# Value products of four tiles in one visit, with the side work set in another order

## What is computed

```python
x = x + tanh(g_xattn) * xattn(layernorm(x), ctx, mask)
x = x + tanh(g_ffn)   * ffn(layernorm(x))
...
q, k, v = proj(hs, Wq, bq), proj(at, Wk, bk), proj(at, Wv, bv)   # 16 heads of 16
probs = softmax(clip(where(attend, q @ k.T / 4, -10000), -50, 50))
delta = layernorm(rs * ((probs @ v) @ Wo.T + bo)) * gamma + beta
...
h = silu(bitlinear(x, w1)) * bitlinear(x, w2)                    # width 704
return bitlinear(h, w3)       # bitlinear: rows of the activations rounded to 8 bits, weights ternary
```

## Time and profile before

| what | value |
|---|---|
| median of 3 runs | 1528.89 us (1526.29 to 1529.96) |
| the profiled execution: its own time | 1529.9 us |
| its span, first to last instruction | 1528.1 us, mean granted TensorE clock 0.973 |
| busy in the span: TensorE, weight loads, VectorE, ScalarE, GpSimd | 91%, 80%, 75%, 64%, 29% |
| one batch in the middle (from the scores behind the value products of n = 5 to the same place one batch on) | 44.87 us |

### The profile page before, as it was taken

How to read it: one execution, slowest core, us unless ns; L and a number is a source line. 1 busy time by engine, 2 the same in 40 slices (tenths; PEclk the granted TensorE clock), 3 DMA queues, 4 the chain that set the end, 5 groups by cost and what they waited for, 6 DMA issues and landing times. The chain is left out here.

```text
span 1528.1 us, 48034 instructions
## 1 busy us (share of the span) xinstructions
PE 1394.8 (91%) x19984; PEld 1219.7 (80%) x19984; DVE 1147.5 (75%) x2241; ACT 979.4 (64%) x1634; POOL 444.9 (29%) x759
## 2 busy tenths in 40 slices
PE   6699999999999999999999999999999999999973
PEld 5588888888888888888888888888888888888861
DVE  6557777877777887877787777778777778877753
ACT  2367766666766666666666666666667666666751
POOL 3423332132333222233322223331323332132310
PEclk9699999999999999999999999999999999999985
DMA  7466565665666566666656665656656665665520
GB/s 211 97 148 164 140 155 141 157 159 147 156 149 155 142 162 150 156 152 149 152 142 160 155 161 143 160 142 147 162 149 156 151 155 141 159 154 149 129 48 8
DMA packets 142477, 222.13 MB, mean 145 GB/s; under 512 B 29162, under 2 KB 135598, under 8 KB 142254
## 3 DMA queue, kind: packets, MB, share of 16 engines
q1 hardware_dynamic: 129966, 199.31, 53.8%
q0 software_dynamic: 12288, 19.69, 5.0%
HBM read 54.00 MB, written 3.28 MB: 37 GB/s over the span
## 5 line engine op out<-in xcount | busy, mean ns | idle before, releaser
L545 ACT ACTIVATE e_sb<-sc 121x800 f32<-121x800 f32 (+1 forms) x768 | 639.9, 845 | 470.9 <-PE sc L1187 463.7
L1187 PE MATMUL sc<-q_st,k_st 96*121 96x200 f32 (+1 forms) x3072 | 495.5, 284 | 5.4 <-DMA q_st<-bd_hi 3.9
L1187 PEld LDWEIGHTS sc<-q_st,k_st 96*121 96x121 f32 (+1 forms) x3072 | 409.9, 187 | 53.2 <-issue 29.1
L779 DVE TENSOR_SCALAR e_sb<-e_sb,hi_b 121x1600 f32<-121x1600 f32 (+1 forms) x384 | 401.5, 1046 | 58.9 <-ACT e_sb L545 58.9
L1207 PE MATMUL pvb<-e_sb,v_sb 121*32 121x100 f32 x12288 | 309.3, 253 | 2.6 <-DVE e_sb L779 2.6
L1207 PEld LDWEIGHTS pvb<-e_sb,v_sb 121*32 121x32 f32 x12288 | 265.8, 110 | 48.2 <-issue 21.8
L770 DVE SCALAR_TENSOR_TENSOR k_lo<-cb,bk_c,k_hi 128x484 fp32r<-128x484 f32 (+1 forms) x192 | 134.8, 702 | 169.3 <-ACT k_hi L557 167.0
L1242 PE MATMUL cb<-wv_hi,c_hi 128*121 128x256 f32 (+1 forms) x768 | 228.4, 297 | 25.3 <-DVE k_lo L770 25.2
L1242 PE MATMUL cb<-wv_hi,c_lo 128*121 128x256 f32 (+1 forms) x768 | 217.1, 283 | 0.0
L1242 PE MATMUL cb<-wv_lo,c_hi 128*121 128x256 f32 (+1 forms) x768 | 216.3, 282 | 0.0
L427 POOL TENSOR_SCALAR x_ve<-mv 100x1 f32<-100x1 f32 x32 | 24.9, 777 | 632.6 <-DVE mv L795 632.6
(11 more groups left out here) (139 smaller groups left out, 1579.4 us busy)
## 6 DMA issues: line engine op xcount, KB each, us to landing
k_st<-k_hi SPq DMA_DIRECT2D x512, 121.0 KB, 2.7
c_in<-in_ctxT SPq DMA_DIRECT2D x64, 484.0 KB, 3.7
k_st<-k_lo SPq DMA_DIRECT2D x256, 121.0 KB, 2.7
k_st<-k_hi SPq DMA_DIRECT2D x256, 119.0 KB, 2.3
c_in<-in_ctxT SPq DMA_DIRECT2D x32, 476.0 KB, 3.6
k_st<-k_lo SPq DMA_DIRECT2D x128, 119.0 KB, 2.3
q_st<-bd_hi POOLq DMA_DIRECT2D x256, 50.0 KB, 3.1
q_st<-bd_lo POOLq DMA_DIRECT2D x128, 50.0 KB, 3.0
```

The costliest lines, as they stand in the source:

```text
L545: nc.scalar.activation(e_sb[n % NE][0:TL[n], k * SW:(k + 1) * SW].rearrange("p (o c) -> p o c", o=2), sc[q % NSC][0:TL[n], :, 0:2 * PW], A ...
L779: V.tensor_scalar(e, e, E_LO, hi_b[b.par][0:TL[n], n:n + 1], ALU.max, ALU.min).then_inc(clip_done, 1)
L1187: last = T_.matmul(sc[q % NSC][0:TL[n], e // 2, (e % 2) * PW:(e % 2 + 1) * PW], k_st[st_slot(b, n // TPC)][:, pr // NQ, pr % NQ, t0:t0 + T ...
```

## The change

Three things are altered; the arithmetic is the same.

1. **Visits of four.** VISIT = 4: attend() calls pv for the tiles n-5 to n-2 at n = 1, 5 and 9, three times per batch in place of six. The newest tile in a visit is two behind, as before. The last batch has four tiles left over in place of two. The buffer of a tile is now named by e_slot(b, n), which with twelve tiles and six buffers gives the same buffers as n % 6.
2. **Side work on TensorE** now stands between the first context half and the value products of its step (in front of scores(n, 1)), not at the step's end: delta at n = 3, x_turn 4, x_query 5, x2_turn 7 (before: 6), up (first gate half) at n = 9 ahead of the visit, its partner behind the visit, and the other two at n = 10 and 11. h_turn and down keep their places.
3. **Side work on the other engines.** ScalarE takes the item (k_head or v_out) ahead of exps(n, 0), and h_turned, x_turned and x_query one step earlier, with the copies of the up products following their matmuls. VectorE takes q_head and q_rest one step earlier, the first hidden_gate at n = 10, and the second half of the hidden part (hidden_gate, hidden_up, h_max to h_quant) at n = 0 of the next batch, around and behind the clip of tile 11. Before, it was at n = 11, ahead of that clip.

```diff
--- before.py
+++ after.py
@@ -85,6 +85,7 @@
     NE = 6
+    VISIT = 4
     NKS = 2
@@ -98,7 +99,7 @@
     INF_TO = 10000.0
-    assert NT % NE == 0 and (STEPS * NT) % NSC == 0 and NB % 2 == 0 and NB >= 8
+    assert 2 * NT % NE == 0 and (STEPS * NT) % NSC == 0 and NB % 2 == 0 and NB >= 8
     assert all(c % 2 == 0 for c in CL) and STEPS * SW == EW
@@ -248,6 +249,9 @@
 
+        def e_slot(b, n):
+            return (NT * b.par + n) % NE
+
         def st_slot(b, u):
@@ -542,7 +546,7 @@
                     act.wait_ge(pv_done, TILE.after(b, n) - NE)
-                nc.scalar.activation(e_sb[n % NE][0:TL[n], k * SW:(k + 1) * SW].rearrange("p (o c) -> p o c", o=2),
+                nc.scalar.activation(e_sb[e_slot(b, n)][0:TL[n], k * SW:(k + 1) * SW].rearrange("p (o c) -> p o c", o=2),
                                      sc[q % NSC][0:TL[n], :, 0:2 * PW],
@@ -621,23 +625,23 @@
                 for n in range(NT):
-                    exps(b, n, 0)
-                    if prev2 and n == 2:
-                        h_turned(b.plus(-2))
-                    if nxt and n == 5:
-                        x_turned(c)
-                    if nxt and n == 6:
-                        x_query(c)
-                    if prev and n == 7:
-                        x2_turned(d)
-                    if prev and n in (8, 10):
-                        ffn_gate(d, (n - 8) // 2)
-                    if prev and n in (9, 11):
-                        ffn_up(d, (n - 9) // 2)
                     if n < ITEM + 1 and own:
...
                         ctx_item(c, n - (ITEM + 1))
+                    exps(b, n, 0)
+                    if prev2 and n == 1:
+                        h_turned(b.plus(-2))
+                    if nxt and n == 4:
+                        x_turned(c)
+                    if nxt and n == 5:
+                        x_query(c)
+                    if prev and n == 7:
+                        x2_turned(d)
+                    if prev and n in (9, 10):
+                        ffn_gate(d, n - 9)
+                    if prev and n in (9, 11):
+                        ffn_up(d, (n - 9) // 2)
                     exps(b, n, 1)
@@ -775,7 +779,7 @@
                     dve.wait_ge(pool_x, X_P.after(b, "mask"))
-                e = e_sb[n % NE][0:TL[n], :]
+                e = e_sb[e_slot(b, n)][0:TL[n], :]
                 V.tensor_scalar(e, e, E_LO, hi_b[b.par][0:TL[n], n:n + 1], ALU.max, ALU.min).then_inc(clip_done, 1)
@@ -975,27 +979,31 @@
                             x_aggr(c)
-                        if n == 7:
-                            q_rest(c)
+                        if n == 6:
+                            q_head(c)
+                    if prev2 and n == 0:
+                        hidden_gate(b.plus(-2), 1)
                     if prev:
...
                             attention_out(d)
-                        if n == 9:
+                        if n == 10:
                             hidden_gate(d, 0)
-                        if n == 11:
-                            hidden_gate(d, 1)
                     if n:
...
                     if nxt and n == 6:
-                        q_head(c)
+                        q_rest(c)
                     if nxt and n % 4 == 1:
...
                             v_guard(c if n > ITEM else b, w // 4, w % 4 - 2)
+                    if prev2 and n == 0:
+                        hidden_up(b.plus(-2), 1)
+                        for step in (h_max, h_scale, h_round, h_quant):
+                            step(b.plus(-2))
                     if prev2 and n == 2:
@@ -1023,12 +1031,6 @@
                             hidden_up(d, 0)
-                        if n == 11:
-                            hidden_up(d, 1)
-                            h_max(d)
-                            h_scale(d)
-                            h_round(d)
-                            h_quant(d)
 
@@ -1132,7 +1134,10 @@
                 clip(e, NT - 1)
-                result(e.plus(-1))
+                hidden_gate(e.plus(-1), 1)
+                hidden_up(e.plus(-1), 1)
+                for step in (h_max, h_scale, h_round, h_quant, result):
+                    step(e.plus(-1))
                 for step in (attention_read, sums_inverse, attention_out, delta_out, delta_stats, delta_aggr,
@@ -1198,7 +1203,7 @@
                         pe.wait_ge(dve_post, D_V.after(b.plus(-1), "z1"))
-                e = e_sb[n % NE]
+                e = e_sb[e_slot(b, n)]
                 for a in range(2):
@@ -1312,8 +1317,8 @@
                 for n in range(NT):
-                    pair = [(b, i) if i >= 0 else (d, i + NT) for i in (n - LAG - 1, n - LAG)]
-                    has_pv = n % 2 == 1 and (n >= LAG + 1 or prev)
+                    group = [(b, i) if i >= 0 else (d, i + NT) for i in range(n - LAG - VISIT + 1, n - LAG + 1)]
+                    has_pv = n % VISIT == 1 and (n > VISIT or prev)
 
@@ -1325,19 +1330,14 @@
                         if has_pv:
-                            for pb, pn in pair:
+                            for pb, pn in group:
                                 pv(pb, pn, 0, first)
...
                     context(0)
-                    attend()
-                    if prev2 and n == 1:
-                        h_turn(b.plus(-2))
                     if prev2 and n == 2:
                         down(b.plus(-2))
-                    scores(b, n, 1)
-                    context(1)
                     if nxt:
@@ -1346,14 +1346,21 @@
                             delta(d, prev2)
-                        if n == 6:
+                        if n == 7:
                             if nxt:
...
                             x2_turn(d)
-                        if n in (7, 9):
-                            up(d, (n - 7) // 2, 0)
-                        if n in (8, 10):
-                            up(d, (n - 8) // 2, 1)
+                        if n in (9, 10):
+                            up(d, n - 9, 0)
+                        if n == 11:
+                            up(d, 1, 1)
+                    attend()
+                    if prev2 and n == 1:
+                        h_turn(b.plus(-2))
+                    if prev and n == 9:
+                        up(d, 0, 1)
+                    scores(b, n, 1)
+                    context(1)
 
@@ -1392,7 +1399,7 @@
                 batch(e, True, False, True, True)
-                for n in (NT - 2, NT - 1):
+                for n in range(NT - VISIT, NT):
                     pv(e, n, 0)
```

## The result

The changed kernel takes **1438.76 us** (median of 4, 1438.57 to 1440.48) against 1527.59 for the kernel before on the same chip: a ratio of 0.942 (95% interval 0.9403 to 0.9436), 5.8% faster. I had written 1474, with a range of 1447 to 1502. So the direction is right, and the gain is some 90 us where 55 were expected, outside the range.

What follows compares the result with a forecast made beforehand. TensorE's own pace plus 2.2 us idle per batch bounds the kernel; after the change VectorE's chain sets the first half. 27.35 + 15.7 = 43.05 us per batch against 44.88, 55 us off 1529.9, median 1.0 lower: 1474 us, range 1447 to 1502.

Steps and rivals of the forecast that it cites:

- What a visit costs: TensorE's pv visits: 21.3 ns per record plus a fixed 0.33 us per visit; three fewer save 1.0 us per batch.
- VectorE, first half: VectorE's chain from tile 11's exponential (0.6 us after first scores) to result(b-2), ending 13.55; continued to k_lo, 27.35.
- TensorE, at delta: TensorE wants to start delta at 12.4 us but waits about 1.2 us for result(b-2), until 13.55.
- Second half: From the value item of n = 7 to the next batch: 15.7 us in place of 18.01.
- Sum: Whole batch: 27.35 + 15.7 = 43.05 us against 44.88, so 1.8 us less, 55 us over 30 batches.
- The two terms: The batch's two parts: 27.35 us to the value item of n = 7, then 15.7 to the next batch.
- I set these against each other: Ends of the run: 1 to 2 us more in the tail, offset by batch 1's shorter version of the gain.
- TensorE alone: Rival: TensorE alone decides and delta doesn't wait; 3.2 us less per batch, 1433 us, or 1453 with half; chance 0.14.
- More waits in the three steps without a visit: Rival: tight ScalarE work and stacking DMAs cost 0.5 to 1.4 us per batch, 1490 to 1516 us; chance 0.17.
- No fixed part: Rival: a visit's 1.52 us has no fixed part; 0.32 us less gain per batch, 1484 us; chance 0.05.
- Slower: Rival: tile 11's exponential ends late, delaying VectorE's chain through mb; 2.4 us later gives 1548 us; chance 0.09.

Runs made afterwards that it cites:

- Experiment 2: The kernel before with visits of four tiles (VISIT = 4) and the side work in its old order: 1495.86 us, ratio 0.9799.
- experiment 1: The changed kernel with VISIT = 2, so the new order of side work alone, six visits per batch: 1507.46 us, ratio 0.988 to the kernel before.
- experiment 4: The changed kernel with VectorE's result(b-2) moved ahead of the clip of tile 1 at n = 2: 1438.23 us, ratio 0.9421 to the kernel before.
- experiment 6: The changed kernel with extra VectorE work at n = 2 or n = 7: two copies 1444.07 or 1438.95 us, one reciprocal 1479.64 or 1438.63 us.
- experiment 5: The changed kernel with result(b-2) ahead of the clip of tile 1, and x_stats and x_aggr moved to n = 0: 1400.91 us, ratio 0.9188.
- experiment 7: The changed kernel with ScalarE's item (k_head, v_out) back behind the side copies, ahead of exps(n, 1): 1650.79 us, ratio 1.0828 to the kernel before.

## Why the prediction came out too small

**"What a visit costs": right.** Fixed price 0.33 us. Experiment 2 gives 0.33 per visit, and a visit of four takes 2.90 us to the next start (684.43 to 687.33), which is 128 x 0.0213 + 0.17. At the 25 ns that the page "TensorE: Matmul & The Clock Gate" of the Trainium skill (Part 1) gives as the least distance of two matmuls, the 128 alone would take 3.2 us (an estimate from the page's figure); the trace has less and decides. The 21.3 ns are a mean, too: the records start in fours, one for each 32 partitions of pvb, 5 to 8 ns apart, with some 65 ns from one four to the next. Another page of the Trainium skill, "TensorEngine Tiling (Array Packing)" (Key Properties), says that TensorE drains when its tiling mode changes. The fixed 0.16 to 0.17 behind a visit of two, three or four tiles fits with it, though no run shows that this is the cause; the page gives no duration.

**"VectorE, first half": right in mechanism, and the joins within 0.2 us.** The exponential at 0.60 was predicted at 0.6, c_hi 4.62 (4.6), attention_read 7.86 (7.95), result 12.97 (13.05), delta_out 16.15 (16.3), first_sum 19.91 (20.1). From there to k_rest it was 6.34 in place of 6.50. The end is 27.03 in place of 27.35.

**"TensorE, at delta": right.** A new wait for result(b-2), with delta at 13.60 (predicted 13.55). I had 1.2 us for it, and it is 0.74, since TensorE came at 12.86 rather than 12.4. A wait for k_lo at n = 3 is in front of it, which I hadn't seen: it holds that value item up by 0.31 (692.26 to 692.99, 0.42 without a wait), of which the bracket shows 0.15. With delta fixed by VectorE this changes nothing.

**"Second half": the term 15.7 was mis-sized; it is 15.18.** Three parts, which the rows show but no run took apart. Two up products now stand beside the visit: the two with the visit between them take 3.50 us from 671.32 to the scores at 674.82, of which the visit is 2.89, so 0.61 for the two, some 0.16 less than at their old places. x2_turn cost 0.09 to the scores behind it (666.76 to 666.85), and these are somewhat slower (0.48 to the value item, 667.33, for 0.41), about 0.16 in all, where I took 0.25. The wait for k_lo with its restart was nearer 0.67 than 0.5. Together that is 0.42 of the 0.52; the rest I didn't place.

**"Sum": the step that failed most in size.** The two terms miss 0.32 and 0.52 us, 0.84 per batch, always to the same side. The rest is in "I set these against each other", the ends set to nothing. Result's y_out marks the batches on VectorE (32 of them; the first line gives first and last start, the others are the 29th and the 31st). First the changed kernel, then the one before:

```profile
L957 DVE SCALAR_TENSOR_TENSOR y_out<-mb,tiny,x x32: 475/479/484, 145.0 to 1429.5; 100x256 f32<-100x256 f32 x32
...
1327.65 0.48 DVE L957 SCALAR_TENSOR_TENSOR y_out<-mb,tiny,x 100x256 f32<-100x256 f32 x1
1402.23 0.48 DVE L957 SCALAR_TENSOR_TENSOR y_out<-mb,tiny,x 100x256 f32<-100x256 f32 x1 [2.77 <-PE mb L1313]
```
```profile
L953 DVE SCALAR_TENSOR_TENSOR y_out<-mb,tiny,x x32: 475/478/485, 154.7 to 1520.8; 100x256 f32<-100x256 f32 x32
...
1410.77 0.48 DVE L953 SCALAR_TENSOR_TENSOR y_out<-mb,tiny,x 100x256 f32<-100x256 f32 x1
1493.50 0.48 DVE L953 SCALAR_TENSOR_TENSOR y_out<-mb,tiny,x 100x256 f32<-100x256 f32 x1 [3.97 <-PE mb L1308]
```

From the first to the 29th, 28 batches, it is 1182.7 us after and 1256.1 before: 73.4 gained, 2.6 each, where I had 28 x 1.83 = 51. Up to the first mark it is 9.7, and over the next two, 1327.65 to 1402.23 against 1410.77 to 1493.50, it is 8.1. The last stretch is equal (27.3 us in both), so the loss of 1 to 2 us in the tail didn't come. 73.4 + 9.7 + 8.1 is 91 us, the difference of the spans. Of the 36 us that I was short, 22 are in the steady batches and 14 at the ends, where the first and last batches gain more than a full one does (my sum had 3.7 for the two batches at the ends). By TensorE's first scores of each batch: batch 0 gains 4.4 us, batch 1 5.9, the 29 behind them 2.6 each, and the last batch with the drain 4.5. In batch 1 the kernel before also had a stretch at the lower clock (mean 0.963), and the changed one had none.

**The rivals.** "TensorE alone" gave 1433, and the measured 1438.8 is near it. Its mechanism is not what happened, though: delta waits, and experiments 1, 4 and 6 show VectorE's chain in charge, in experiment 1 up to delta. That its number is near is luck: its 96 us were 3.2 per batch for the middle alone, while the middle gave 2.6 per batch and the ends some 14 us beyond my sum. The rival's mechanism became true in experiment 5, at 1401, not at 1433. "More waits in the three steps without a visit" is hardly in the trace: in the middle of the span scores never wait for e_sb, and twice in 32 batches for k_st, for the stacking DMAs that this rival named. These two waits, 0.21 and 0.31 us at the first scores of a batch (428.28 and 1061.88), cost nothing in the end, since the batch that follows is shorter by as much or more (41.84 and 41.72 us). "No fixed part" fell with experiment 2. "Slower" rightly said that a delay on this chain counts in full; in experiment 7 it was k_hi behind two copies that was late, not the exponential of tile 11, and in the changed kernel nothing was.

**Open.** Why an up product beside a visit is cheaper by 0.16 than behind a key half wasn't measured by itself, nor were the terms of the ends. A few batches of each run are about 0.35 us longer than the others; two of them in the changed kernel end in the waits for k_st above, of the rest I have no account. What the lower clock costs in experiments 1 and 7 was read from the lengths of their batches; no run separates it. Visits of six weren't tried; they would need more buffers for e_sb.

## What to carry to other kernels

- Between two engines that meet at fixed points, add up each one's work from join to join. The longer sum sets that stretch, whatever the busy shares say: a VectorE at 79% of the span, and 87% of that stretch, set 27 of 42 us here while TensorE was busy 97% of it, and 1.4 us on its chain cost 41 us in one half of the batch and nothing in the other.
- Movable work of the bottleneck engine belongs into the stretch that another engine sets; there it replaces waiting. Two tiles more in the first half cost 1.1 us in the old order and 0.1 in the new one. Visits of three put those tiles into the other half, which together with a wait of 1.0 us ate the whole gain.
- Ahead of a long uninterruptible piece on one engine, the others' in-order queues must issue what feeds the chain before what waits for that piece: one item behind the copies hT and bd cost 212 us. And where a prediction sums a middle and sets the ends to nothing, count the ends too.

## What the runs showed of the hardware

- TensorE's clock fell to 0.55 for a stretch of 3.6 us behind waits of 2.39 and 0.74 us (experiment 7). With waits of 1.30 and 0.76 (experiment 1) it fell to 0.50 for 3.42 us, in twelve of 29 batches; in the others, with waits like these, it stayed at 1.00. In the changed kernel, with waits of 0.15 and 0.74, it stays at 1.00 in all of them.
- On VectorE two 100x256 tensor_scalar with constants start 0.20 us apart though each shows 0.28 to 0.29; a reciprocal of the same size takes 1.74 (experiment 6).
- Records of 32 columns and 100 moving columns start 21.3 ns apart on average in visits of two, three and four tiles: in fours, mostly 5 to 8 ns apart, and some 65 ns from one four to the next.
